# Group x3 of a fused graph network: transposed by TensorE, or moved as 32 by 32 blocks and turned by VectorE

## Time and profile before

| | |
|---|---|
| median of 3 runs | 919.82 us (918.21 to 920.14) |
| the profiled execution, its own time | 921.33 us |
| its span in the trace | 919.5 us |
| TensorE busy | 885.8 us, 96% |
| VectorE / ScalarE / GpSimd busy | 664.0 / 564.0 / 339.1 us |
| granted TensorE clock, mean | 0.994 of full |
| share of the 16 DMA engines | about 12% |

### The profile page before, as it was taken

The page is one execution under the profiler, slowest core; times in us unless marked ns, Lnnn a source line. Parts: engine busy times, 40 slices in busy tenths (PEclk is TensorE's granted clock), DMA queues, the critical chain, the costliest instruction groups (busy, mean ns, idle before and its releaser), DMA issues.

```text
span 919.5 us, 14510 instructions
## 1 busy us (share of the span) xinstructions
PE 885.8 (96%) x4966; PEld 768.8 (84%) x4966; DVE 664.0 (72%) x1583; ACT 564.0 (61%) x1233; POOL 339.1 (37%) x550
## 2 busy tenths in 40 slices
PE   8999999988989999999999999999999999999996
PEld 6888985466877799888989998898989899978986
DVE  5988886886687766667677667767676777665744
ACT  5676766935755674677377547745763775466341
POOL 3777875621023520342153136214421631340221
PEclk9999999999999899999999999999999999999999
DMA  5412201320110101012001201010120001001000
GB/s 188 148 60 71 74 29 69 138 70 1 35 59 1 35 12 47 1 47 65 5 13 35 70 1 36 24 58 1 47 69 1 12 12 47 1 11 36 1 24 23
DMA packets 26594, 38.54 MB, mean 42 GB/s; under 512 B 3333, under 2 KB 12422, under 8 KB 26010
## 3 DMA queue, kind: packets, MB, share of 16 engines
q1 hardware_dynamic: 26088, 36.05, 11.7%
q10 hardware_dynamic: 434, 1.57, 0.5%
HBM read 21.89 MB, written 15.73 MB: 41 GB/s over the span
## 4 chain that ended last, share of the span: by engine, by line
PE 47%; DVE 12%; ACT 8%; POOL 7%; issue 5%; ACTq 0%; DVEq 0%; POOLq 0%
PE psum L141 14%; PE psum L143 13%; PE psum L142 13%; PE psum L1892 2%; PE psum L1893 2%; ACT gate L1465 2%; PE psum L1896 2%; POOL out_rstd L1398 1%; DVE x_stats L1644 1%; DVE x L1666 1%; DVE in_h L1634 1%; POOL node_l L1416 1%; POOL x_rstd L1398 1%; ACT raw L1496 1%; ACT gate L1468 1%
## 5 line engine op out<-in xcount | busy, mean ns | idle before, releaser
L1465 ACT ACTIVATE gate<-psum,gate_bias 128x256 f32<-128x256 f32 (+2 forms) x296 | 143.4, 556 | 62.0 <-PE psum L1896 53.0
L141 PE MATMUL psum<-in_h,wih_h 128*128 128x256 f32 (+2 forms) x312 | 106.8, 342 | 7.3 <-DVE in_l L1638 5.0
L143 PE MATMUL psum<-in_h,wih_l 128*128 128x256 f32 (+2 forms) x312 | 103.5, 332 | 0.0
L142 PE MATMUL psum<-in_l,wih_h 128*128 128x256 f32 (+2 forms) x312 | 102.8, 329 | 0.0
L1432 POOL TENSOR_TENSOR gate<-in_h,in_l 128x512 f32<-128x512 f32 x14 | 17.9, 1307 | 157.5 <-DVE in_l L1638 157.5
L141 PEld LDWEIGHTS psum<-in_h,wih_h 128*128 128x128 f32 x312 | 58.8, 188 | 19.2 <-DVE in_l L1638 9.1
L1468 ACT ACTIVATE gate<-cell 128x512 f32<-128x512 f32 (+2 forms) x80 | 40.3, 503 | 51.2 <-DVE cell L1622 39.7
L1619 DVE TENSOR_TENSOR gate<-gate 128x256 f32<-128x256 f32 (+2 forms) x48 | 24.0, 501 | 61.3 <-ACT gate L1465 61.2
L142 PEld LDWEIGHTS psum<-in_l,wih_h 128*128 128x128 f32 x312 | 59.0, 189 | 5.5 <-issue 0.5
L143 PEld LDWEIGHTS psum<-in_h,wih_l 128*128 128x128 f32 x312 | 58.8, 189 | 4.6
L141 PE MATMUL psum<-e_h,shared 128*128 128x384 f32 x180 | 61.4, 341 | 0.2
(11 more groups left out here) (403 smaller groups left out, 2887.2 us busy)
## 6 DMA issues: line engine op xcount, KB each, us to landing
x_spill<-x SPq DMA_DIRECT2D x30, 256.0 KB, 2.0
xt<-in_x_t_dram SPq DMA_DIRECT2D x16, 256.0 KB, 2.6
raw<-x_spill SPq DMA_DIRECT2D x16, 256.0 KB, 2.9
o_spill<-xt SPq DMA_DIRECT2D x14, 256.0 KB, 2.0
xt<-o_spill SPq DMA_DIRECT2D x14, 256.0 KB, 3.3
x<-x_spill SPq DMA_DIRECT2D x14, 256.0 KB, 3.5
out_dram<-raw SPq DMA_DIRECT2D x14, 256.0 KB, 2.3
raw<-in_adj_t_dram ACTq DMA_DIRECT2D x1, 1024.0 KB, 9.2
```

The lines of the kernel that those rows point to most:

```text
L141: pe.matmul(dst, lh, rh, start=start, stop=False, **kw)
L142: pe.matmul(dst, lh, rl, start=False, stop=False, **kw)
L143: return pe.matmul(dst, ll, rh, start=False, stop=stop, **kw)
L1465: nc.scalar.activation(gate[q][:, 0:n], banks[GATE_BANK[q]][:, 0:n], ACT.Tanh if q == 2 else ACT.Sigmoid, bias=gate_bias[:, p - 1, q:q + 1 ...
```

## The change

For groups 1 to 6 (`moved`), twelve graphs in all, x3t leaves TensorE. Instead:

- x3move_j (SyncE): when x3 is normalized and the buffer `turning` is free, 16 DMAs from SBUF to SBUF. DMA (a, b) takes, from the 32 partitions b of x3, the 32 features a of each of the four tiles (runs of 128 bytes), to the 32 partitions a of `turning`. It stands before norm_0 in slot 2 of SyncE's list, and alone in slot 5 for j = 1.
- x3turn_j (VectorE): one 128x512 transpose in place, of 32 by 32 blocks, when all 16 have landed. It stands last in slot 2 and in slot 6.
- x3high_j: ScalarE's copy to power 0's high part and VectorE's subtraction, now from `turning` in SBUF, stand behind power2 (slots 3 and 7). So on ScalarE and VectorE they leave slots 2 and 6.
- TensorE: no transposes; power1 waits for its two banks itself, power2 waits for nothing more, coefs0 still waits for all three low parts.

Group 0 and group 7 keep TensorE's transposes. Some semaphores are merged elsewhere, with the same order.

The diff, cut to its core:

```diff
@@ -1030,6 +1030,9 @@
         th, tl = late[:, 0:BABY, :], late[:, BABY:2 * BABY, :]
         x3h, x3l = (late[:, 2 * BABY + i, :].rearrange("p (t d) -> p t d", d=D) for i in range(2))
         gh, gl = sb("gh", [P, NT, GB, D], F32R), sb("gl", [P, NT, GB, D], F32R)
+        turning = sb("turning", [P, N])
+        quarters = 4
+        quarter = P // quarters
         later_h = [in1_h[:, 0:N], in1_h[:, N:2 * N], in2_h[:, 0:N]]
         later_l = [in1_l[:, 0:N], in1_l[:, N:2 * N], in2_l[:, 0:N]]
...
@@ -1093,12 +1096,17 @@
                 return in2_h[:, 0:N], in2_l[:, 0:N]
             return gat_h[:], gat_l[:]
 
+        def moved(g):
+
+            return not isinstance(g, int) or 1 <= g < G - 1
+
         def conv_of(n, conv):
...
@@ -1217,19 +1225,19 @@
                    ["gather1_0", "x3t_1", "power1a_1", "power1b_1"], ["weight1_0", "power2_1"], ["gather0_1"],
                    ["weight0_1", "coefs0_1"], ["coefs1_1", "gather1_1", "inner_0", "weight1_1", "hturn", "inner_1"]]
         FILL_ACT = [[], ["x3norm_0", "x3split_0", "evens_h"], ["x3t_0", "norm_0"],
-                    ["power1_0", "power2_0", "evens_l", "out_0", "gather0_0"], ["rest_h", "coefs0_0", "prep_1", "weight0_0", "x3norm_1"],
-                    ["coefs1_0", "x3split_1", "rest_l"], ["gather1_0", "x3t_1", "norm_1"], ["power1_1", "out_1", "power2_1"],
+                    ["power1_0", "power2_0", "evens_l", "x3high_0", "out_0", "gather0_0"], ["rest_h", "coefs0_0", "prep_1", "weight0_0", "x3norm_1"],
+                    ["coefs1_0", "x3split_1", "rest_l"], ["gather1_0", "x3t_1", "norm_1"], ["power1_1", "out_1", "power2_1", "x3high_1"],
                     ["input_0", "gather0_1"], ["weight0_1", "coefs0_1"],
                     ["coefs1_1", "gather1_1", "ahead_0", "inner_0", "input_1", "inner_1"]]
-        FILL_DVE = [[], ["ysum_1", "ysum_0", "turn_0"], ["x3t_0", "x3sum_1", "outsum"], ["power1_0", "power2_0", "gather0_0"],
-                    ["coefs0_0", "weight0_0"], ["turn_1", "coefs1_0"], ["gather1_0", "x3t_1"], ["power1_1", "weight1_0", "power2_1"],
+        FILL_DVE = [[], ["ysum_1", "ysum_0", "turn_0"], ["x3t_0", "x3sum_1", "outsum", "x3turn_0"], ["power1_0", "power2_0", "x3high_0", "gather0_0"],
+                    ["coefs0_0", "weight0_0"], ["turn_1", "coefs1_0"], ["gather1_0", "x3t_1", "x3turn_1"], ["power1_1", "weight1_0", "power2_1", "x3high_1"],
                     ["gather0_1", "input_0"], ["weight0_1", "coefs0_1"],
                     ["coefs1_1", "gather1_1", "innersum_0", "weight1_1", "x3add", "input_1", "innerlow_0", "innersum_1", "x3first", "innerlow_1"]]
         FILL_POOL = [[], ["x3split_0", "turn_0"], ["norm_0", "outsum", "x3sum_1"], [], [], ["x3split_1", "turn_1"], ["norm_1"], [], [], [],
                      ["whole", "x3first"]]
-        FILL_SP = [["prep_1"], [], ["norm_0"], ["out_0"], ["ahead_0"], [], ["norm_1"], ["out_1"], ["x3load"], [], []]
+        FILL_SP = [["prep_1"], [], ["x3move_0", "norm_0"], ["out_0"], ["ahead_0"], ["x3move_1"], ["norm_1"], ["out_1"], ["x3load"], [], []]
         LSTM_NAMES = ("evens_h", "evens_l", "rest_h", "rest_l", "hturn", "whole", "x3load", "x3add", "x3first", "x3early")
-        L3_NAMES = ("x3sum", "x3norm", "x3split", "x3low", "x3t", "power1a", "power1b", "power1", "power2", "coefs0",
...
@@ -1346,6 +1354,17 @@
                 sp.wait_ge(x2_ready, n + 1)
                 sp.dma_start(x2_dram[n], flat(x2[j])).then_inc(x2_stored[j], 16)
 
+            def x3move(g, j):
+                if not moved(g):
+                    return
+                n = GB * g + j
+                sp.wait_ge(x3_ready, n + 1)
+                sp.wait_ge(power_lo[1 - j], BABY * (g + j))
+                for a in range(quarters):
+                    for b in range(quarters):
+                        rows = turning[quarter * a:quarter * (a + 1), :].rearrange("k (t b i) -> k t b i", b=quarters, i=quarter)[:, :, b, :]
+                        sp.dma_start(rows, x3[quarter * b:quarter * (b + 1), j, :, quarter * a:quarter * (a + 1)]).then_inc(x3_moved, 16)
+
             def out_piece(g, j):
...
@@ -1531,17 +1550,20 @@
                 n = GB * g + j
                 act.wait_ge(x3_ready, n + 1)
                 if not at_end(g, j):
-                    need(act, power_done[1 - j], BABY * (g + j))
+                    need(act, power_done[1 - j], (BABY - 1) * (g + j))
                 nc.scalar.copy(x3_parts(g, j)[0][:], x3[:, j, :, :]).then_inc(x3_hi, 1)
 
             def x3t(g, j):
-                act.wait_ge(power_done[j], BABY * g + 1)
+                act.wait_ge(x3_turned, GB * g + j + 1)
                 if not at_end(g, j):
                     need(act, coef_done, NT * (GB * g + j))
-                nc.scalar.copy(powers(g, j)[0][0], product_banks(g, j)[j][:]).then_inc(power_hi[j], 1)
+                source = turning if moved(g) else product_banks(g, j)[j]
+                nc.scalar.copy(powers(g, j)[0][0], source[:]).then_inc(power_hi[j], 1)
 
             def power(g, j, k):
-                act.wait_ge(power_done[j], BABY * g + k + 1)
+                act.wait_ge(power_done[j], (BABY - 1) * g + k)
+                if k == 1 and moved(g):
+                    need(act, coef_done, NT * (GB * g + j))
                 nc.scalar.copy(powers(g, j)[0][k], product_banks(g, j)[(j + k) % 2][:]).then_inc(power_hi[j], 1)
 
             def coefs(g, j, half):
...
@@ -1699,13 +1722,22 @@
                 need(dve, x3_ready, GB * g + j + 1 - GB)
                 (spread_of if g == G - 1 else stats_of)(x3_norm[j], [x3[:, j, t, :] for t in range(NT)], x3_asked)
 
+            def x3turn(g, j):
+                if moved(g):
+                    n = GB * g + j
+                    dve.wait_ge(x3_moved, 16 * quarters * quarters * (n - GB + 1))
+                    nc.vector.transpose(turning[:], turning[:]).then_inc(x3_turned, 1)
+
             def x3t(g, j):
-                dve.wait_ge(power_hi[j], BABY * g + 1)
+                dve.wait_ge(power_hi[j], BABY * g + (BABY if moved(g) else 1))
                 high, low = powers(g, j)
-                nc.vector.tensor_tensor(low[0], product_banks(g, j)[j][:], f32(high[0]), ALU.subtract).then_inc(power_lo[j], 1)
+                source = turning if moved(g) else product_banks(g, j)[j]
+                if moved(g):
+                    dve.wait_ge(x3_turned, GB * g + j + 1)
+                nc.vector.tensor_tensor(low[0], source[:], f32(high[0]), ALU.subtract).then_inc(power_lo[j], 1)
 
             def power(g, j, k):
-                dve.wait_ge(power_hi[j], BABY * g + k + 1)
+                dve.wait_ge(power_hi[j], BABY * g + (k if moved(g) else k + 1))
                 high, low = powers(g, j)
                 nc.vector.tensor_tensor(low[k], product_banks(g, j)[(j + k) % 2][:], f32(high[k]), ALU.subtract).then_inc(power_lo[j], 1)
 
...
@@ -1951,14 +1986,20 @@
                     pe.wait_ge(coef_lo, NT * n)
                 for t in range(NT):
                     mm = pe.transpose(tile(product_banks(g, j)[j][:], t), x3[:, j, t, :], ident[:])
-                mm.then_inc(power_done[j], 1)
+                mm.then_inc(x3_turned, 1)
 
             def power(g, j, k, tiles=range(NT)):
                 n = GB * g + j
                 high, low = x3_parts(g, j)
                 pe.wait_ge(x3_lo, n + 1)
-                if k > 1:
-                    pe.wait_ge(power_lo[j], BABY * g + k - 1)
+                if not moved(g):
+                    if k > 1:
+                        pe.wait_ge(power_lo[j], BABY * g + k - 1)
+                elif k == 1:
+                    if j == 0:
+                        pe.wait_ge(y_summed, 2 * g)
+                    else:
+                        pe.wait_ge(coef_lo, NT * n)
                 for t in tiles:
                     mm = matmul3(pe, product_banks(g, j)[(j + k) % 2][:], (high[:, t, :], low[:, t, :]),
                                  (pow_h[k - 1][:, t, :], pow_l[k - 1][:, t, :]), t == 0, t == NT - 1)
```

More of the change, by code:

```diff
@@ L498, in _ @@
             exp_logits(3)
-            act.wait_ge(bias_spread, 1)
+            act.wait_ge(pe_setup, NT + 1)
             for i in range(2):
@@ L865, in _ @@
             pe.wait_ge(c_w, 48)
-            pe.matmul(tile(banks[3][:], 0), ones[0:1, :], bias0[:], start=True, stop=True).then_inc(bias_spread, 1)
+            pe.matmul(tile(banks[3][:], 0), ones[0:1, :], bias0[:], start=True, stop=True).then_inc(pe_setup, 1)
             pe.wait_ge(weights_ready, 1)
@@ L1094, in gathers @@
             return gat_h[:], gat_l[:]
+        def moved(g):
+            return not isinstance(g, int) or 1 <= g < G - 1
         def conv_of(n, conv):
             return GB * conv + n + 1 if at_start(n) else 2 * n + conv + 1
-        lws_ready, bcols_zero, vpad_zero, weff_done, k_chain = (
-            sem(k) for k in ("lws_ready", "bcols_zero", "vpad_zero", "weff_done", "k_chain"))
+        x3_moved, x3_turned = sem("x3_moved"), sem("x3_turned")
+        lws_ready, cleared, weff_done, k_chain = (
```

(19 more changed lines are left out.)

6 lines of the change are left out of this document (3 added, 3 removed).

## The result

| | before | after |
|---|---|---|
| median, 20 runs each | 919.85 us | 923.38 us |
| range of the runs | 917.66 to 921.74 | 921.69 to 929.06 |
| ratio, 95% interval | | 1.0055 (1.0039 to 1.0071) |
| profiled execution: own time, span | 921.33, 919.5 us | 929.06, 927.3 us |
| TensorE busy, instructions | 885.8 us, x4966 | 886.9 us, x4918 |

The change is slower, by 0.4 to 0.7%. The forecast (no change) was wrong; the first rival, the blocks that land too late, was right about the place of the loss. The executions after fall into two groups, 13 of 921.7 to 923.7 and 7 of 927.2 to 929.1, and the profile shown here is of the upper one. So its span is not set against the median; a profile of the lower group (experiment 9) stands beside it.

The account below looks back on a forecast made before the run. Steps alternate between a TensorE leg and one set by the other engines, which holds the transposes. Five steps at 0 and step 7 at -0.2 gave 921.1 us profiled; forecast median 919.6, range 917.0 to 924.5.

Parts of the forecast that it names:

- the first rival: Before x3turn_0 in slot 2: blocks land too late, cell 3 queues behind on VectorE; 924.5 to 928 us, chance 0.18.
- The bound: Each step: about 44 us bound by TensorE, about 40 by the other engines, both transpose slots in the latter; gain 0.
- The prediction's sign of being right: On TensorE: 48 instructions fewer, busy time down by 13 us, span unchanged.
- The moves of the first graph: SyncE's 16 DMAs in slot 2: issues 0.48 apart, last landing 9.4 us after x3 is ready; cost 0.
- The turn: VectorE's 128x512 transpose at the end of slot 2: taken as 0.7 us, bounds 0.3 and 1.3.
- The upper bound, 0.68: SyncE's moves: largest distance between issues, 0.64 and a gap, last landing 12.4 us after x3 is ready.
- the cover of 2 us: Slot 2 on VectorE, before cell 3's product: time the nearest rows left before late blocks would lengthen the step.
- The packets: DMA engines, each graph's moves: 27 ns a packet, 3.9 us an engine, beside issues of 7.6, so not the limit.
- The limit of the first rival: Slot 2: blocks landing over 11.6 us after x3 is ready cost a microsecond each, in each of 6 steps.
- The late low part: Before coefs0_0: power 0's low part comes 0.6 later; TensorE's wait takes back the transposes' gain, net 0 five times.
- The race: Slot 5: VectorE's state subtraction going before GpSimd's would gain about 0.7 x 5 = 3.5, giving 916.1; chance 0.06.
- The estimate of 1.24: VectorE's turn: four 128x128 bf16 transposes of 311 ns by the Trainium skill, 1.24 us, still inside the cover.

Follow-up runs that it names:

- experiment 9: The change itself run once more, unaltered, to profile another execution: 923.17 us, ratio 1.0040 to the kernel before.
- experiment 4: The change with the same packets in 8 DMAs of 64 partitions per graph instead of 16 of 32 (blocks misplaced): 919.55 us, ratio 0.9999.
- experiment 1: The change with only the second graph of each of the six groups moved, the first keeping TensorE's transposes: 919.97 us, ratio 1.0009.
- experiment 5: The change with 16 DMAs per graph, each of 32 runs of 512 bytes instead of 128 of 128: 923.33 us, ratio 1.0038.
- experiment 8: Kernel before with ScalarE's x3split_1 copy behind rest_l, plus both graphs moved in 8 DMAs each (blocks misplaced): 915.65 us, ratio 0.9958.
- 7: Kernel before with ScalarE's x3split_1 copy behind rest_l, plus only the second graph of each group moved: 915.15 us, ratio 0.9958.
- 12: Repeat of 7, the second graph moved and x3split_1 behind rest_l: 915.15 us, ratio 0.9958 to the kernel before.
- experiment 11: Repeat of 6, the kernel before with x3split_1 behind rest_l and nothing moved: 915.44 us, ratio 0.9956.
- experiments 3: The change with groups 1 to 5 moved and group 6 keeping TensorE's transposes: 923.87 us, ratio 1.0029 to the kernel before.
- experiments 2: The change with only the first graph of each of the six groups moved: 923.71 us, ratio 1.0047 to the kernel before.
- experiment 10: The change plus ScalarE's x3split_1 copy put behind rest_l: 922.77 us, ratio 1.0030 to the kernel before.
- 6: Kernel before, nothing moved, with one edit: ScalarE's x3split_1 copy goes behind rest_l in slot 5: 916.86 us, ratio 0.9969.

## Why the prediction was wrong

- **The bound** (two legs, the transposes in the one that other engines set): right. All transposes gone and nothing late gives 0.9999 (experiment 4); the second graph alone gives 1.0009 and a wait longer by 0.40 at cell 7 (experiment 1). The busy share of 96% and the row's 272 ns were no guide: TensorE's busy time rose by 1.1 us with 48 instructions fewer in the first profile, and fell by 3.6 (882.2) in experiment 9, which has less of the lower clock. The prediction's sign of being right, busy time down by 13 us, was wrong by its own reading: it counts 272 ns for each, where the text allows 0.44 for four, 5.3 in all.
- **The moves of the first graph: here it failed.** The step was "issues without a wait follow each other by 0.48", taken from loads. Measured: 0.64, and in seven of the twelve series one issue held for 1.05 to 1.68, so 12.2 us to the last landing in step 3 and not 9.4: 2.4 of the difference is the distance, 0.7 the one long issue, and the landing gave 0.25 back (1.85 for 2.1). The turn (0.71 for 0.7) was right. The upper bound, 0.68 from the earlier trace rows, held for the distance between ordinary issues but not for a whole series: its 12.4 was passed in steps 5 and 7 (12.6 and 12.5). It should still have been the value, as the moves were the one kind of transfer that no row showed, and the cover of 2 us was thinner than the spread between the bounds (16 issues times 0.2). What holds one issue back isn't shown.
- **The packets** (27 ns each, not the limit): right. Neither twice as many for an issue (experiment 4, 0.66 apart) nor a quarter as many, four times as long (experiment 5, 0.63), changed the issues' pace by more than 0.02. So the Trainium skill's rule on less than 512 bytes (DMA: Bandwidth & Descriptors, "Specifications") decides nothing here; no run shows what a small packet costs by itself.
- **The limit of the first rival**, 11.6 us, each microsecond beyond it costing one in six steps: right in kind. By it, 12.2 us cost 0.6 x 6 = 3.6 us; the median went up by 3.5. That the two agree is luck, for the parts differ: five steps lost 0.2 to 0.4 each in the mean, less than 0.6, and step 7 lost 3.1 or more. In steps 3 to 6 the limit was about 12.0 and not 11.6 (TensorE, without its transposes, comes 0.44 earlier, which is argued and not tested alone). Of 16 such steps in the profiles of the change, 9, 3 and 5, the four whose first series landed after less than 12.0 us took 83.6 to 83.7, as before, and the twelve that landed after 12.2 to 12.8 took 83.9 to 84.5. A series without a long issue lands after 11.5, so in these steps it is the one long issue that costs. In step 2 a series that landed after 11.7 already cost 0.2 (83.8 to 83.9 against 83.6), and in step 7 the limit is tighter still: cell 4 starts 35.8 us after the mark before, 37.5 with the change, 35.3 in experiment 4. There the late turn (1.7) and TensorE's earlier arrival (0.4) add up to one wait longer by 2.1, and behind it the granted clock fell.
- **TensorE's clock in step 7** stood nowhere in the prediction. Seven executions were at 927 to 929, beyond the range; in the one pair of profiles, step 7 has half of what sets them apart, 2.8 us.
- **The late low part** before coefs0: right, a wait of about 0.3 before coefs0 (seen in experiments 4 and 8). It is free while the other engines set the pace; with TensorE the limit, steps 2 to 6 take 414.1 with it (experiment 8) and 413.4 or 414.0 without (7 and 12).
- **The race** was a real item of the size that it was given, 0.7 a step (0.6 in experiment 11), but from an edit of its own. The change did not flip it. Its working was off: with the transposes in place it left TensorE only 0.2 before it is the limit, and the edit alone gained three times that; where the rest lay isn't shown. The Trainium skill's rule (SBUF — State Buffer, "SBUF: two separate sides") is borne out by it: with GpSimd's instruction behind, the same VectorE instruction takes 0.52 and not 1.58.

## What to carry to other kernels

Before an instruction is taken off the engine with the highest busy share, read the chain of waits in order of time at its very place: if the chain is elsewhere there, and the engine runs dry a few microseconds later, the removal only lengthens that wait. A transfer split into many small ones is priced by the issues of its queue, from a row of the same kind of transfer or else by the highest price in the trace with a reserve for an issue that is held, and its wait must not stand ahead of critical work on an in-order engine. And look for two engines that exclude each other on the chain: exchanging two names in one list was worth 0.3 to 0.4%, where 48 transposes fewer were worth nothing.

## What the runs showed of the hardware

- An issue of a transfer within SBUF held SyncE mostly for 0.59 or 0.60 us, 0.64 from start to start, and nearly the same in the other two shapes: 0.66 for 64 partitions and 256 runs (experiment 4), 0.63 for 32 runs of 512 bytes (experiment 5). In seven of the change's twelve series one issue took 1.05 to 1.68. A store to DRAM took 0.32 to 0.47 in the kernel before, and 0.59 or 0.60 where it followed on 16 moves.
- VectorE's transpose of 32 by 32 blocks took 0.71 us for 128x512 in float32, no more than a subtraction of that size (0.68). The estimate of 1.24 that the prediction worked out from the Trainium skill (VectorE: DVE Perf Modes, "The three transpose paths") was too high.
- TensorE's granted clock fell to 1.2 GHz behind the wait before cell 4 of step 7, up to which the engine had been busy: for some 3.4 us where the wait was 2.1 (experiments 3, 4, 7, 8 and 12) and also where it was 4.0 to 4.4 (experiments 2, 5 and 9), for some 6.8 us where it was 3.7 (experiment 10) and 4.2 (the change's first profile). In the profiles of before and of experiments 1, 6 and 11 it stayed at 2.4 GHz behind the same 2.1.
